# First-pass scores of a non-local block issued image by image on two row tiles, with the scans reading and writing their lines in place

## What is computed

```python
# non-local block, N = 1024 positions, 32 inner channels, 8 images
theta = einsum('kc,bcn->bkn', w_theta, xf)
phi   = einsum('kc,bcn->bkn', w_phi, xf)
g     = einsum('kc,bcn->bkn', w_g, xf)
attn  = softmax(einsum('bkn,bkm->bnm', theta, phi), axis=-1)
y     = einsum('bnm,bkm->bkn', attn, g)
out   = einsum('ck,bkn->bcn', w_last, y).reshape(B, C, H, W) + x

# four scans: down, up (over rows), right, left (over columns)
def step(carry, x):
    new = x + relu(conv1d(carry, w, b))      # 9 taps, 64 -> 64 channels
    return (new, new)
```

## Time and profile before

| | us |
|---|---|
| median of 3 runs | 1628.1 (1627.47 to 1633.12) |
| the profiled execution | 1628.84 |
| its span, first to last instruction | 1627.1 |

### The profile page before, as it was taken

The page is one execution under the profiler, slowest core; times in us unless marked ns, Lnnn a source line. Parts: engine busy times, 40 slices in busy tenths (PEclk is TensorE's granted clock), DMA queues, the critical chain, the costliest instruction groups (busy, mean ns, idle before and its releaser), DMA issues. The chain is left out here.

```text
span 1627.1 us, 25795 instructions
## 1 busy us (share of the span) xinstructions
PE 1440.0 (89%) x9714; PEld 977.4 (60%) x9714; DVE 680.8 (42%) x963; ACT 563.2 (35%) x913; POOL 137.8 (8%) x243
## 2 busy tenths in 40 slices
PE   4888997887887799999988999999999999958767
PEld 1335225776776699999985555555555555537544
DVE  3664013113112677777753333332333323326562
ACT  2654674223223443434343222222222212214250
POOL 5000002930000111111100000000000000003000
PEclk9555897999998999999999999999999999979977
DMA  4900000000000500000000000000000000040001
GB/s 98 104 1 1 1 1 3 0 0 0 0 0 21 186 0 0 0 0 0 0 1 1 0 0 0 0 0 0 0 0 0 0 0 0 0 100 5 1 1 52
DMA packets 34241, 23.48 MB, mean 14 GB/s; under 512 B 24621, under 2 KB 28749, under 8 KB 34205
## 3 DMA queue, kind: packets, MB, share of 16 engines
q1 hardware_dynamic: 33837, 21.92, 6.2%
q10 hardware_dynamic: 368, 1.07, 0.3%
HBM read 20.80 MB, written 2.18 MB: 14 GB/s over the span
## 5 line engine op out<-in xcount | busy, mean ns | idle before, releaser
L948 PE MATMUL sp_f<-hankel,sp_ut 128*128 x2304 | 420.9, 344 | 0.0
L948 PEld LDWEIGHTS sp_f<-hankel,sp_ut 128*128 128x128 f16 x2304 | 222.8, 98 | 216.7 <-issue 27.5
L987 ACT COPY sp_sums<-sp_f 64x1023 f32<-64x1023 f32 x128 | 129.0, 1008 | 427.6 <-PE sp_f L948 427.6
L1010 DVE COPY sp_sums<-sp_f 64x1024 f32<-64x1024 f32 x128 | 155.2, 1212 | 91.9 <-PE sp_f L948 91.9
L1008 DVE COPY sp_mix<-mix 128x512 f32 x64 | 27.3, 427 | 281.6 <-PE sp_f L948 281.6
L959 PE MATMUL sp_o<-sp_sums,sp_mix 128*64 128x128 f32 (+2 forms) x1024 | 123.7, 392 | 0.0
L193 PE MATMUL nl_ps<-mix 32*128 32x512 f32 x256 | 94.2, 1065 | 22.0 <-ACT nl_spent L289 22.0
L388 PE MATMUL convh<-runningh,toeplitz 128*128 128x128 f32 x610 | 85.9, 287 | 15.2 <-DVE runningh L405 15.2
L388 PE MATMUL convv<-runningv,toeplitz 128*128 128x128 f32 x610 | 85.8, 287 | 15.2 <-DVE runningv L405 15.2
L316 DVE TENSOR_REDUCE nl_max<-nl_ps 128x1 f32<-128x1024 f32 x64 | 74.0, 1218 | 43.3 <-PE nl_ps L193 43.3
L388 PEld LDWEIGHTS convh<-runningh,toeplitz 128*128 128x128 f32 x610 | 74.4, 192 | 26.7 <-DVE runningh L405 26.7
(11 more groups left out here) (299 smaller groups left out, 1828.4 us busy)
## 6 DMA issues: line engine op xcount, KB each, us to landing
hankel<-phi_rows SPq DMA_DIRECT2D x32, 256.0 KB, 6.0
ex_w<-in_L_ffn_weight SPq DMA_DIRECT2D x1, 2080.0 KB
m_plus<-in_L_ffn_M_phi_plus SPq DMA_DIRECT2D x2, 1024.0 KB, 14.0
m_minus<-in_L_ffn_M_phi_minus SPq DMA_DIRECT2D x2, 1024.0 KB, 16.3
out<-x SPq DMA_DIRECT2D x8, 256.0 KB, 3.3
x<-in_x SPq DMA_DIRECT2D x1, 1024.0 KB, 8.5
x<-in_x ACTq DMA_DIRECT2D x1, 1024.0 KB, 12.4
ar<-in_L_ffn_M_u SPq DMA_DIRECT2D x2, 192.0 KB, 3.1
```

The costliest lines, as they stand in the source:

```text
L948: mm = nc.tensor.matmul(f_ps[b][:, lo:(half + 1) * BANK], ut[:, hu, b, i, :, :].rearrange("p a c -> p (a c)"), m.hankel[:, hf, ds(j * 2 + ...
L987: nc.scalar.copy(sums[n][HALF[1], b, 1:T], f_ps[b][HALF[1], 0:T - 1]).then_inc(f_act, 1)
L1010: nc.vector.tensor_copy(sums[n][HALF[0], b, :], f_ps[b][HALF[0], :]).then_inc(f_dve, 1)
```

## The change

The lines of the non-local part, of the set-up and of both scans are rewritten.

1. **Set-up.** x comes in four DMAs of 512 KB, behind the small weights, with a semaphore for each half of the images; the block no longer waits for it. PE runs 24 matmuls on the identity. `rows` is cleared later, in the non-local part, and `cols` not at all.
2. **First pass.** The second half of phi (`phi_b`) and all of theta (`theta_b`) are copied once to the row tile two places further. An image's left bank is multiplied on its own row tile, its right bank on the far one. The slots are no longer tied to `im`; two pairs of slots alternate, and each image waits for its own slot alone. `values` now stands behind the first two images. DVE cuts the maxima into pieces, for the first four images in the middle of the pass.
3. **Second pass.** The shift holds the maximum alone. The sums are inverted, widened, turned by PE (`turn_scale`) and multiplied onto the heads on DVE. No logarithm is taken. In a unit, the shift of the first two images now stands ahead of the scores, that of the other two behind them. The turning of the second four images' shift is put into units 2 and 6.
4. **Scans.** The two copying stages are gone. The horizontal scan fetches its lines from `rows` (two copies a line), and on its way back writes them into x (four copies a line). POOL writes the first and the last column.

The diff, cut:

```diff
+            @block.tensor
+            def _(pe):
+                pe.wait_ge(ident_ok, 1)
+                for n in range(WARM):
+                    mm = nc.tensor.matmul(warm_ps[:, :], m.ident[:, :], m.ident[:, :], start=True, stop=True)
+                mm.then_inc(warm, 1)
...
+        def slots(s):
+            n = s + 1 if s else 0
+            return ps[2 * (n % 2)], ps[2 * (n % 2) + 1]
...
+                for g in range(2):
+                    nc.gpsimd.tensor_copy(theta_b[HALF[1 - g], 1, :], theta[1][HALF[g], :]).then_inc(q_pool, 1)
...
+                    nc.gpsimd.tensor_copy(phi_b[HALF[1 - g], 1, :], phi[1][HALF[g], BANK:T]).then_inc(q_pool, 1)
...
+                    for j, im in enumerate((2 * pair, 2 * pair + 1)):
+                        if s >= 3:
+                            pe.wait_ge(ex_ok, 2 * s - 3 + j)
+                        nc.tensor.matmul(slots(s)[j][:, 0:BANK], theta[q][rows_of(im), k * P:(k + 1) * P], phi[q][rows_of(im), 0:BANK], start=True, stop=True)
+                        far = rows_of((im + 2) % QUAD)
+                        nc.tensor.matmul(slots(s)[j][:, BANK:T], theta_b[far, q, k * P:(k + 1) * P], phi_b[far, q, :], start=True, stop=True).then_inc(s_ok, 1)
...
+                    shifted(0, True)
...
+                    for im in range(QUAD):
+                        mm = nc.tensor.matmul(out[im], phi[q][rows_of(im), k * P:(k + 1) * P], theta[q][rows_of(im), c * BANK:(c + 1) * BANK],
+                                              start=(im >= 2), stop=(im < 2))
+                        if im == 1:
                             mm.then_inc(t_ok, 1)
+                    shifted(1, False).then_inc(t_ok, 1)
...
+                score(0)
+                values()
+                for s in range(1, PAIRED):
+                    score(s)
+                pe.wait_ge(cut_ok, 1)
+                pe.wait_ge(ex_ok, ROWS - 2)
+                turn_shift(0, 0, ps[3][:, 0:BANK])
+                turn_shift(0, 1, ps[3][:, BANK:T]).then_inc(turn_ok, 1)
...
-                act.wait_ge(ex_ok, ROWS)
-                nc.scalar.activation(rest[:, :, :, :], rsum[:, :, :, :], ACT.Ln).then_inc(ln_ok, 1)
...
+                    nc.vector.reciprocal(inv, rsum[:, q, :, :]).then_inc(cut_step, 1)
...
+                    nc.vector.tensor_tensor(heads[w % 2][:, :], y_ps, scale_t[w % 2][:, :], ALU.mult).then_inc(y_c, 1)
...
+    def fetch(self, copy, dst, pair, par):
+        for hp in range(2):
+            last = copy(dst[HALF[hp], :, :], self.column(pair, par, hp))
+        return last
...
+    def store(self, copy, line, pair, par):
+        for hp in range(2):
+            for p in range(2):
+                last = copy(self.token(pair, par, hp, p), line[HALF[hp], p::2, :])
+        return last
...
-            rows_to_cols_stage(nc, m)
-            conv_passes(nc, m, m.cols, 2, "h")
-            cols_to_tokens_stage(nc, m)
+            vertical_passes(nc, m, mixing_step)
+            horizontal_passes(nc, m)
```

More of the change, by code:

```diff
@@ L79, in _ @@
                                         base=0, pattern=[[-1, P]], channel_multiplier=1).then_inc(ident_ok, 1)
[L80 to L85, removed]
+                pool.wait_ge(ident_ok, 1)
                 for p in range(2):
@@ L111, in nonlocal_stage @@
     ROWS = NQ * NB * QUAD
+    PAIRED = ROWS // 2
     UNITS = NQ * NH * NB
@@ L411, in _, with fetch, step @@
                 act.sem_inc(saved, 1)
-                def fetch(line, odd):
-                    nc.scalar.copy(added[odd][:, :, :], at(line)).then_inc(fetch_ok, 1)
-                def step(n, odd, line, ahead=None):
+                def fetch(pair, odd, back):
+                    (lines.refetch if back else lines.fetch)(nc.scalar.copy, added[odd][:, :, :], pair, odd).then_inc(fetch_ok, 1)
+                def step(n, odd, pair, back):
                     act.wait_ge(line_ok, n + 1)
-                    nc.scalar.copy(at(line), running[odd][:, :, PADP:PADP + PAIRS]).then_inc(saved, 1)
-                    if isinstance(ahead, int) and ahead >= 2 * TOP - 3:
-                        act.wait_ge(saved, n + 1)
-                    if ahead is not None:
-                        fetch(ahead, odd)
+                    (lines.store if back else lines.keep)(nc.scalar.copy, inner(running[odd]), pair, odd).then_inc(saved, 1)
@@ L463, in cols_to_tokens_stage @@
[L463 to L479 removed]
+                    step(n, n % 2, (2 * FWD - n) // 2, True)
@@ new lines, in vertical_passes, with horizontal_passes, ends, _ @@
+def vertical_passes(nc, m, mixing_step):
+    conv_passes(nc, m, RowLines(m), 0, "v", lambda block, saved, n: spectral_mixing(nc, m, block, mixing_step))
+def horizontal_passes(nc, m):
+    lines = ColumnLines(m)
+    def ends(block, saved, n):
+        @block.gpsimd
+        def _(pool):
+            for hp in range(2):
+                for p in range(2):
+                    src = m.rows[HALF[0], hp::2, p::2, PADP:PADP + 1].rearrange("c r g a -> c g (r a)")
+                    nc.gpsimd.tensor_copy(lines.token(0, 0, hp, p), src)
+            pool.wait_ge(saved, n)
+            lines.store(nc.gpsimd.tensor_copy, lines.at(W // 2 - 1, 1), W // 2 - 1, 1)
+    conv_passes(nc, m, lines, 2, "h", ends)
```

396 lines of the change are left out of this document (238 added, 158 removed).

## The result

The changed kernel takes **1563.7 us** (median of 4 runs, 1560.04 to 1565.55), the kernel before beside it 1628.3 (1627.47 to 1633.12). The ratio is 0.9595, 95% interval 0.9569 to 0.962. The profiled execution took 1562.97 with a span of 1561.1, 66.0 less than the span before.

What follows compares the result with a forecast made beforehand. The largest touched stage, the first pass, was taken as bound by a latency loop, not an engine. 1628.8 - 55.1 + 10.2 - 12.1 + 0.9 - 1.5 + 0.5 = 1571.7, 1571.0 against the median; 1563 to 1579 (65%), 1560 to 1590 with rivals (92%).

Steps and rivals of the forecast that it cites:

- seam behind it: Between first and second pass: shift turned, copied (1.3) and added with scores (1.6), without logarithm or values; first exponential at 110.8.
- First pass, loop: First pass: single-image waits and two row tiles give 1.155 us an image, 73.9 us for 64 images instead of 119.4.
- Start: Set-up to values: warm-up ends at 10.3, projection starts at 14.2, values take 8.9 us, maxima run from 35.0.
- Rival 1: Values and seam: the clock stays low, values take 13.9 us instead of 8.9, seam 1 us more; 1577 us; 15%.
- Second pass: Second pass: split shift makes PE the bound, unit 2.56 instead of 2.46; with added turns and output steps +10.2 us.
- Scans: Both scans: copying stages go, -12.1 us; extra fetches and stores +0.9; clock -1.5 with the norm; backward steps +0.5.
- Rival 2: Backward horizontal scan: ACT bounds it, 30 steps up to 0.45 us longer each; 1584 us; 12%.
- My 0.20 spacing: Backward horizontal scan: ACT's four stores spaced 0.20 us apart, stores and fetch done in 1.2 us and hidden.
- The clock gain that I counted at the norm: First steps behind the shorter PE pauses may keep the full clock; 1.5 us back, counted together with the horizontal scan.
- Rivals 3 and 4: First pass: images don't overlap, 1613 us, 5%; or an image's two matmuls don't overlap either, 1715 us, 3%.
- (4): First pass: an image's two matmuls don't overlap, 3.41 us an image on PE alone; slower, 1715 us; 3%.
- The rule on the clock: First pass: by the skill page, keeping PE in use gives full clock, 1.5 us more gain; the earlier trace spoke against.

Runs made afterwards that it cites:

- e1: Changed kernel, but in the first pass both images of a slot pair wait for both exponentials of that pair, as before; 1583.3 us.
- e3: Changed kernel with both first-pass edits undone: pairs wait for pairs, and each image's two matmuls share one row tile; 1608.4 us.
- e6: Changed kernel, but in the second pass the shift stands behind the scores for all four images; 1570.6 us.
- e4: Changed kernel with the horizontal scan as before: both copying stages restored, whole lines in the scan; 1571.3 us.
- e8: Changed kernel, but in the backward loops of both scans ScalarE's fetch stands ahead of the store; 1560.7 us.
- e2: Changed kernel, but each image's two first-pass score matmuls go to its own row tile, one after the other; 1592.3 us.
- e5: The changed kernel run once more without edits, on the same chip as e6 and e8; 1564.9 us.
- e9: Changed kernel without the 48 warm-up matmul records of the first block; 1561.0 us.
- e11: e10 without the warm-up matmuls; 1558.6 us.
- e10: Changed kernel with the backward fetch ahead of the store, and first weight copies waiting only for what they overwrite; 1557.4 us.

## Why the prediction was right, and where it was off

| term, us of the span | predicted | measured |
|---|---|---|
| first exponential of the second pass (from 165.96) | 110.8, -55.1 | 106.30, -59.7 |
| ... start of the long run of maxima | 35.0 | 30.76 |
| ... its length | 72.9 | 71.7 |
| ... seam behind it | 2.9 | 3.8 |
| second pass | +10.2 | +0.6 |
| both scans and what lay between and behind them | -12.2 | -9.9 |
| the untouched rest | 0 | +2.9 |
| sum | -57.1 | -66.0 |

In the span the forecast was 8.9 us off, and that is small because part of its errors cancelled: 4.6 in the first row and 9.6 in the second pass were too pessimistic, 2.3 in the scans and 2.9 in the rest went the other way. That the ends met within the range is partly luck. The boundaries are the first exponentials above, the start of the weights (258.35 before, 199.27 after), and the first matmul of the norm. Its rows, before and after:

```profile
524.36 2.90 PE L510 MATMUL centredw<-centre,x 128*128 128x128 f32 x12 [7.79 <-PEq L1723]
```

```profile
455.43 1.92 PE L663 MATMUL centredw<-centre,x 128*128 128x128 f32 x8 [2.75 <-PEq L1877]
```

**First pass, loop: right.** 1.155 an image predicted; 71.7 us for 62 images, less the cut in the middle, which measured 1.0 (1.3 predicted), is 1.14. Four images take 4.52 us where the clock is 1.00, DVE's own pace, and 4.64 where it is 0.50, where the loop of 4.63 binds, as predicted (rows below). e1 to e3 reproduce the loop with each part undone. Of the steps this was the largest and the best founded, because it came from the distances in one period of the earlier trace rows rather than from busy shares.

**Start: right in what happens, 4.2 us too late.** The warm-up ended at 8.9, not 10.3; x had landed by the time the projection could start; the values took 7.33 us, not 8.9. The price of 0.139 a record came from matmuls of 128 columns; these have 64 and cost 0.115. Rival 1, the low clock in the values, did not come in any run.

**Second pass: the step that failed.** It reads: "the part ahead is new: 0.21 for 512 columns at 2.4 GHz, up to 0.33 with the change-over of the row. So PE's unit is 2.50 to 2.62 and PE becomes the bound". The 0.33 behind the scores was kept in full for two shifts, and the two ahead were added to it as new work. Measured: 0.31 behind, 0.02 to 0.10 for the part ahead, a unit of 2.33, and by e6 the new order gains 2.5 to 4.0 us, where I had put a cost of 3.2. PE did become a bound, as I wrote, but at 2.29 and level with the loop. The first two units, which are longer in both kernels, gave another 1.4 (6.3 instead of 7.7 us), a term that I didn't have. The added steps were near: a unit with `turn_scale` is longer by about 1.05, so four cost 4.2 (4.8 predicted), and the two shift turns 0.35 each (0.6).

**Scans: the mechanism was there, of the smaller size.** The stages went (the two gaps of e4 are 12.0 longer, where 12.1 out, 0.9 in and 1.5 of clock were predicted), and the filter behind the first gap kept its clock, as in only three of the eleven profiled executions without the copying stages. Rival 2 happened in part: the fetch is late by a little in every second step, 29 intervals of 1.946 instead of 1.866, 2.3 us instead of 0.5; e8 removes exactly that. My 0.20 spacing for the four stores was too short: they take 1.23 together, 0.31 apart. The clock gain that I counted at the norm did not come; its first matmuls ran at 0.54 (455.4 to 459.1). Where the clock falls between the scans and the norm differs between executions of the same code, so the 1.5 was a bet and not a term.

**Rivals 3 and 4.** At 1.14 us an image both fell. For (4) e2 says more: two matmuls of an image on one row tile, behind each other, cost 1.58 an image and not 3.41, so even that way round the kernel stays faster than before.

**The rule on the clock.** I let the old row speak against it, and after the change the row changed. DVE and the clock in stretches of the first pass of the changed kernel (columns: length, PE busy, PEld, DVE, ACT, POOL, clock, DMA share, GB/s), and every fourth exponential, at 0.50 and then at 1.00:

```profile
40.00:45.00 5.00, 5.00 (x22) 2.31 (x20) 4.98 (x6) 4.91 (x10) 0.00 (x0) 0.50 1.41 163
50.00:65.00 15.00, 14.86 (x56) 3.92 (x52) 15.00 (x15) 15.00 (x28) 0.00 (x0) 1.00 1.37 157
```

```profile
40.05 1.11 ACT L357 ACTIVATE nl_spent<-nl_ps,nl_max 128x1024 bf16<-128x1024 f32 x1
...
44.69 1.11 ACT L357 ACTIVATE nl_spent<-nl_ps,nl_max 128x1024 bf16<-128x1024 f32 x1
...
50.34 1.11 ACT L357 ACTIVATE nl_spent<-nl_ps,nl_max 128x1024 bf16<-128x1024 f32 x1
...
54.87 1.11 ACT L357 ACTIVATE nl_spent<-nl_ps,nl_max 128x1024 bf16<-128x1024 f32 x1
```

Four images take 4.64 at 0.50 (40.05 to 44.69) and 4.53 at 1.00 (50.34 to 54.87): the busy shares of DVE hardly show it, but at the lower clock the loop binds, and the full clock gives 0.11. The length of the run of maxima follows: 71.5 us in e6, where the clock was low for 10 us of it, 71.7 here, 72.3 in e5, where it was low from 37 to 82 us, and 72.9 in e9, where it was low from 33 us to the end. So the two views differ by about 1.5 us, as I had reckoned (my product, 64 x 0.02, is 1.3; with the unrounded 0.025 it is 1.6). The Trainium skill, page "TensorE: Matmul & The Clock Gate", section "Part 1: The HAM clock gate (the "warmup" mystery)", says that activity releases the throttle. The traces agree only in part: the changed kernel's pass is at 1.00 in parts, but at other times in each execution, and e2's pass, with a fuller PE row, stays at 0.50 (last section). Neither my row of before nor the rule told how much of the pass would be at the full clock.

**The untouched rest** is where a forecast of this kernel ends. From the first variance of the norm to the end of the span the profiled executions took 1098.9 (e6) to 1106.7 us (e1), 1103.1 as changed, 1100.0 in e4 and in the kernel before, with the same code. So the +2.9 of the table is not shown to come from the change. The spectral matmuls in it agree within 0.6 us; what differs lies in the start of the window attention and in the last stage. I have not shown what sets it beyond this: in the changed kernel the granted clock falls to 0.5 twice before the windows run steadily.

```profile
479.00:483.00 4.00, 4.00 (x20) 3.85 (x20) 0.56 (x1) 0.17 (x1) 0.00 (x0) 0.52 0.13 48
483.00:487.00 4.00, 1.42 (x12) 1.23 (x11) 2.84 (x4) 1.54 (x2) 1.06 (x4) 0.91 0.00 0
487.00:491.00 4.00, 2.95 (x14) 2.60 (x14) 2.41 (x4) 0.60 (x1) 0.00 (x0) 0.50 0.00 0
```

## What to carry to other kernels

Take a pipeline's period from one turn of its rows and write down each hand-over: the same sum then prices every variant (5.77, 6.33 and 7.46 us here), and the part that matters may be a wait for a pair rather than any engine's work. When work is reordered on one engine, ask what of it is new: moving a piece ahead of the hand-over added at most 0.1 us to PE here, and took the piece out of the loop. A clock level that one trace shows behind a pause may not be there in the next execution, so a term that lives on it is a range and not a number. And where a slow engine both stores and fetches, the fetch that the next step needs goes first.

## What the runs showed of the hardware

- **A full PE row does not mean the full clock.** In e2 PE was busy without a pause from 35 us to the end of the first pass, and the clock stayed at its lower level from 36 us on. One stretch of it:

```profile
85.00:95.00 10.00, 10.00 (x27) 5.95 (x26) 7.51 (x7) 8.29 (x14) 0.00 (x0) 0.50 0.00 0
```

  The changed kernel, with the two matmuls of an image on two row tiles at once, had stretches at 1.00 with PE no busier in the row (50 to 65 us above), and they lay at other times in e5. Why it rises in one and not in the other stays open.
- **A granted clock of 1.00 at the very start need not be a reading.** In e9 the view prints 1.00 from the start, though six projection records took 2.56 us in one stretch and sixteen took 3.00 in the next (columns: length, PE busy, clock, DMA share, GB/s):

```profile
9.00:12.00 3.00, 2.56 (x6) 1.00 1.02 275
12.00:15.00 3.00, 3.00 (x16) 1.00 1.07 196
```

  The trace of e9 has no record of the clock ahead of 12.1 us (e11: 14.9, the changed kernel: 5.0), and the view prints 1.00 where none is. Up to there a projection record took 0.43 us; in e10, at 1.00 throughout, 32 took 7.09, 0.22 each. e11, whose first record comes 2.8 us later than e9's, needs 9.76 us for the same projection instead of 8.39.

- **Small matmuls.** 64 records of 64 columns in f32 took 7.33 us at the full clock, 0.115 each, against 0.139 for 128 columns: half the columns save a sixth. At the lower clock the kernel before needed 0.217 for each of them.
